# A first load cut into six transfers, a first head in six banks, and two convolution heads multiplied before the first turn

## The reference

```python
qkv = jnp.einsum('bsh,hf->bsf', x, w_qkv)            # 16 heads of 128 columns, q, k and v
scores = jnp.einsum('bhqd,bhkd->bhqk', q, k) / sqrt(128)
probs = softmax(scores)
values = jnp.einsum('bhqk,bhkd->bhkd', probs, v)     # column sums of probs times v
x = layernorm(x + einsum('bsf,fh->bsh', values, w_o))

kv = jnp.einsum('bhil,bhjl->bijhl', ctx, ctx)        # 16 heads of 8 channels
y = irfft(rfft(kv, 2L) * rfft(ssm_kernel, 2L))[..., :L] + kv * D
out = jnp.einsum('bijhl,bhil->bjhl', y, x)
x = layernorm(x + out)
```

## Time and profile before

| | us |
|---|---|
| median of 3 runs | 962.76 (962.2 to 966.51) |
| the profiled execution | 965.18 |
| its span | 963.4 |
| PE busy | 883.9 |
| DVE busy | 618.2 |

### The profile page before, as it was taken

The page is one execution under the profiler, slowest core; times in us unless marked ns, Lnnn a source line. Parts: engine busy times, 40 slices in busy tenths (PEclk is TensorE's granted clock), DMA queues, the critical chain, the costliest instruction groups (busy, mean ns, idle before and its releaser), DMA issues. The chain is left out here.

```text
span 963.4 us, 14009 instructions
## 1 busy us (share of the span) xinstructions
PE 883.9 (92%) x4408; PEld 633.9 (66%) x4408; DVE 618.2 (64%) x1169; ACT 395.9 (41%) x895; POOL 260.1 (27%) x246
## 2 busy tenths in 40 slices
PE   5999999999797799999999799999879889999995
PEld 4788888887444588888888575444454466555554
DVE  3666656666599654554554656888649988555554
ACT  1554565555411333233233322767630046555541
POOL 3122122120395022122212233111048641144200
PEclk9999999999698799999999989999979979999999
DMA  7011101101012111111112200000001013011001
GB/s 280 23 45 44 33 33 44 44 23 55 12 50 69 32 43 49 49 33 49 49 34 67 84 1 1 1 1 1 1 0 47 19 45 145 3 58 58 1 1 44
DMA packets 21752, 40.16 MB, mean 42 GB/s; under 512 B 2544, under 2 KB 13552, under 8 KB 20464
## 3 DMA queue, kind: packets, MB, share of 16 engines
q1 hardware_dynamic: 21712, 39.66, 12.8%
HBM read 38.60 MB, written 1.05 MB: 41 GB/s over the span
## 5 line engine op out<-in xcount | busy, mean ns | idle before, releaser
L1260 PE MATMUL bank<-xTh,ringh 128*128 128x512 f32 x432 | 176.7, 409 | 12.0 <-DVE xTl L873 11.2
L1261 PE MATMUL bank<-xTl,ringh 128*128 128x512 f32 x432 | 173.3, 401 | 0.0
L1262 PE MATMUL bank<-xTh,ringl 128*128 128x512 f32 x432 | 172.3, 399 | 0.0
L1260 PEld LDWEIGHTS bank<-xTh,ringh 128*128 128x128 f32 x432 | 83.1, 192 | 30.5 <-DVE xTl L873 11.2
L1262 PEld LDWEIGHTS bank<-xTh,ringl 128*128 128x128 f32 x432 | 82.4, 191 | 20.0
L1261 PEld LDWEIGHTS bank<-xTl,ringh 128*128 128x128 f32 x432 | 83.1, 192 | 15.3
L851 ACT ACTIVATE SF<-bank 128x512 f32<-128x512 f32 x108 | 64.5, 598 | 60.8 <-DVE HF L1237 30.7
L1237 DVE TENSOR_TENSOR HF<-bank,SF 128x512 f32<-128x512 f32 x96 | 63.5, 687 | 34.8 <-PE bank L1607 31.2
L1077 DVE TENSOR_TENSOR arena<-bank,arena 128x512 f32<-128x512 f32 x48 | 33.2, 691 | 73.0 <-PE bank L1262 73.0
L793 ACT ACTIVATE Eh<-arena 128x512 fp32r<-128x512 f32 x48 | 30.3, 632 | 115.4 <-DVE arena L1081 115.4
L1296 PE MATMUL bank<-outh,Eh 128*128 128x256 f32 x192 | 63.5, 331 | 1.4 <-DVE El L1085 1.4
(11 more groups left out here) (214 smaller groups left out, 2018.7 us busy)
## 6 DMA issues: line engine op xcount, KB each, us to landing
ring<-w_attn SPq DMA_DIRECT2D x16, 384.0 KB, 3.2
ring<-w_moe SPq DMA_DIRECT2D x24, 256.0 KB, 2.7
lowraw<-w_low SPq DMA_DIRECT2D x6, 1024.0 KB, 5.8
toep<-toep SPq DMA_DIRECT2D x32, 128.0 KB, 2.1
outring<-w_down SPq DMA_DIRECT2D x24, 128.0 KB, 2.0
outring<-wo_attn SPq DMA_DIRECT2D x16, 128.0 KB, 2.0
ring<-w_ffn SPq DMA_DIRECT2D x6, 256.0 KB, 5.0
wq<-w_attn SPq DMA_DIRECT2D x1, 1344.0 KB, 13.3
```

Source lines behind the costliest of these rows:

```text
L1260: pe.matmul(o, ringh[:, slot, wc], xTh[:, k, halves[j]], start=(k == 0), stop=False)
L1261: pe.matmul(o, ringh[:, slot, wc], xTl[:, k, halves[j]], start=False, stop=False)
L1262: ins = pe.matmul(o, ringl[:, slot, wc], xTh[:, k, halves[j]], start=False, stop=(k == DK - 1))
```

## The change

1. **Loads.** SP now issues the first half of the tokens of `xT`, then head 0's weights as q, k and v thirds with a semaphore each, then the second half of `xT`, then head 0's output weights. `consts` and the skip vector `dskip` move ahead of `xN`.
2. **Splits.** DVE casts and subtracts half by half and signals each of the two feature blocks (`x_high`, `x_low`). ACT casts head 0's weights in thirds, POOL subtracts them in thirds.
3. **First projections.** `project_first` does, for each of the six, the two high x high matmuls first, then the two with `ringl`, then the two with `xTl`, with waits of their own. The order is q, k, v of the first half, then of the second (`FIRST`), into six different banks (`FIRST_BANKS`).
4. **Convolution ahead.** PE does convolution head 0 in the last attention head, between `attn_out(14)` and `key_weights(15, 0)`, and head 1 after `attn_out(15)`, before the turn. POOL multiplies both heads' products as soon as the attention weights are split, into a part of `lowraw` (free until the second layer's feed-forward) instead of `kv`, and then adds the first four diagonals. From head 2 on POOL waits for `xt_act`, i.e. until the turn has ended.
5. **The room for it.** The turn writes banks 4 to 7. The first four `diag` are made by ACT before head 0 of the attention. In the last attention head ACT casts and DVE splits the output weights earlier.

```diff
-            sp.dma_start(xT[:], x_t.rearrange("(k p) t -> p k t", p=P)).then_inc(xt_in, 16)
+            def load_x(j):
+                half = slice(j * HALF, (j + 1) * HALF)
+                sp.dma_start(xT[:, :, half], x_t[:, half].rearrange("(k p) t -> p k t", p=P)).then_inc(xt_in[j], 16)
+            def load_first(part, signal):
+                cols = slice(part * D, (part + 1) * D)
+                sp.dma_start(ring[:, 0, cols], w_attn0[0, :, cols]).then_inc(signal, 16)
+            load_x(0)
+            load_first(0, first_in[0])
+            load_first(1, first_in[1])
+            load_first(2, ring_in[0])
+            load_x(1)
...
-            for h in range(2):
-                conv_fix(h, h)
             pool.wait_ge(ctx_in, 16)
-            pool.wait_ge(out0_banks, 4)
+            for h in range(2):
+                conv_products(0, h, h, cT, cT)
+            for h in range(2):
+                conv_fix(h, h)
             for h in range(CH):
-                conv_products(0, h, h % 2, cT, cT)
+                if h == 2:
+                    pool.wait_ge(xt_act, 4)
+                if h >= 2:
+                    conv_products(0, h, h % 2, cT, cT)
...
-            pe.wait_ge(x_split, 1)
-            for c in range(6):
-                project(0, 0, c)
+            def project_first(c):
+                part, j = c // 2, c % 2
+                o = bank[:, FIRST_BANKS[c], :]
+                pe.wait_ge(hi_first, part + 1)
+                for k in range(DK):
+                    pe.wait_ge(x_high, 2 * j + k + 1)
...
+            for c in FIRST:
+                project_first(c)
...
+                if isinstance(h, int) and h == NH - 1:
+                    pe.wait_ge(act_evac, 4 * NH)
+                    conv(0, 0, 0)
                 key_weights(h, 0)
...
             attn_out(NH - 1, 1)
-            def turn(layer_norm):
+            conv(0, 1, 1)
+            def turn(layer_norm, first_bank=0):
...
-                for h in range(4):
+                for h in range(2 - 2 * layer, 4):
                     conv(layer, h, h)
```

More of the change, by code:

```diff
@@ L723, in head @@
                 high_e(h, 1)
-                high_out(h, slot, out0_done, count(h - 1))
+                if not last:
+                    high_out(h, slot, out0_done, count(h - 1))
                 high_v(h, 0)
@@ L732, in _, with norm_and_turn @@
                 evac_q(0, 0, j)
-            for j in range(2):
                 evac_v(0, 0, j)
+            act.wait_ge(skip0_in, 16)
+            act.wait_ge(const_in, 16)
+            for h in range(4):
+                act.activation(diag[:, h, :], ident, ACT.Identity, scale=dskip[:, h:h + 1]).then_inc(diag_done, 1)
             two_at_a_time(act, NH, head)
-            def norm_and_turn(layer_norm, turn=True, high=False, lead=0):
+            def norm_and_turn(layer_norm, turn=True, high=False, lead=0, first_bank=0):
                 def deviations(j):
@@ L934, in head @@
                 low_e(h, 1)
-                low_out(h, slot)
+                if not last:
+                    low_out(h, slot)
                 scale_v(h, slot, 0)
@@ L1330, in head @@
                 ahead(5)
-            pe.wait_ge(x_split, 1)
-            for c in range(6):
-                project(0, 0, c)
+            def project_first(c):
+                part, j = c // 2, c % 2
+                o = bank[:, FIRST_BANKS[c], :]
+                pe.wait_ge(hi_first, part + 1)
+                for k in range(DK):
+                    pe.wait_ge(x_high, 2 * j + k + 1)
+                    wc = slice(part * D + k * P, part * D + (k + 1) * P)
+                    pe.matmul(o, ringh[:, 0, wc], xTh[:, k, halves[j]], start=(k == 0), stop=False)
+                if part < 2:
+                    pe.wait_ge(lo_first, part + 1)
+                else:
+                    pe.wait_ge(w_split, 1)
+                for k in range(DK):
+                    wc = slice(part * D + k * P, part * D + (k + 1) * P)
+                    pe.matmul(o, ringl[:, 0, wc], xTh[:, k, halves[j]], start=False, stop=False)
+                for k in range(DK):
+                    pe.wait_ge(x_low, 2 * j + k + 1)
+                    wc = slice(part * D + k * P, part * D + (k + 1) * P)
+                    ins = pe.matmul(o, ringh[:, 0, wc], xTl[:, k, halves[j]], start=False, stop=(k == DK - 1))
+                ins.then_inc(proj_done, 1)
+            for c in FIRST:
+                project_first(c)
             pe.wait_ge(ones_done, 1)
```

123 lines of the change are left out of this document (69 added, 54 removed).

## The result

The changed kernel takes 958.20 us (median of 10 runs, 952.77 to 960.63) against 962.77 (10 runs, 959.20 to 966.51) of the kernel before: 0.9946 of it, with 0.9924 to 0.9969 as 95% interval. A second comparison gave 957.79 against 962.33, 0.9939 (0.9918 to 0.9961). (The ratio and its interval are the record's, from all the runs of a comparison; the quotient of the two medians is 0.9953 both times.) So it is faster by about 5 us where 10.4 were forecast, and lies just above the range, which ended at 957.5. The profiled execution took 958.47, its span is 956.7.

A forecast was written before the change was run, and what follows sets the result against it. PE was taken to bound attention, with waits at the start and around the last head and turn. Terms -5.8 - 4.6 + 0.5 - 0.5 = -10.4 us took the profiled 965.18 to 954.8, median 952.4; range 948.0 to 957.5.

The forecast's parts named there:

- Head 2's split: Attention head 0: POOL's split of head 2's weights comes in head 0's time as before; no cost counted.
- POOL's products: Beside heads 14 and 15, 4 x 1.04 us: taken as 0, at most one product's 1.04 us.
- head 0 of the convolution before `key_weights`: Last attention head: three matmuls there put +0.5 us on the chain to the turn.
- The convolution: Behind the turn: 14 heads left for PE, first one cold, ending at 298.1; -4.6 us.
- Rival (c): Convolution: clock is up at head 2 and DVE bounds it, 39.5 us; total 950.2 us; chance 0.15.
- the cold case: Convolution starting at 1.2 GHz: 41.7 us from the turn's end to the last reduction instead of 46.35.
- The start: First projections: input and weights land in pieces, PE starts at 5.4 instead of 11.18; -5.8 us.
- The Trainium skill's figure for small transfers: Start: at 138 GB/s a third takes 0.95 us, PE starts at 6.0; the term would be -5.2.
- The turn: Norm before the turn: `ve` falls from 0.65 to 0.17, -0.5 us; convolution head 1 ahead of it counted 0.
- The forecast's own sign of error: Stages from the experts on: prediction is wrong if they change by over 2 us.
- rival (e): Later stages: further cold stretches of 2.7 us each, six make it slower, 968.6 us; chance 0.02.
- the forecast's step from profile to median (-2.4): Whole kernel: the profiled execution stood 2.4 above the median, so 954.8 became a median of 952.4 us.

The follow-up runs named there:

- Early_w2: The changed kernel with head 2's projection weights issued ahead of `xN`; 956.13 us, 0.9927 of the kernel before.
- split_late: The changed kernel with POOL's split of head 2's weights held until both `El` of head 0 are written; 956.63 us in 12 timed runs, 0.9929.
- quiet_short: The changed kernel with all transfers behind the second input half issued only once that half has landed; 958.2 us in a single run.
- quiet_long: The changed kernel with `xT` in two 4 KB-row transfers, head 0's weights in one, everything else issued after the second input piece landed; 956.5 us, single run.
- conv0_late: The changed kernel with convolution head 0 also behind `attn_out(15)`, with head 1; 955.17 us in one run.
- start_only: The changed kernel with only the new loads, six banks and casts in parts, products and convolutions put back as before; 958.24 us, 0.9965.

## Why the prediction missed

By its own terms, from the table of events (stage lengths, mean of before against mean of after):

| term | forecast | measured |
|---|---|---|
| start, to head 0's scores | -5.8 | -5.1 |
| head 0's chain ("Head 2's split comes in head 0's time as before") | 0 | +1.2 |
| from there to head 15's scores, with POOL's products | 0 | +0.3 |
| head 0 of the convolution before `key_weights` | +0.5 | +0.4 |
| `attn_out(15)` to the turn's end | -0.5 | -1.5 |
| convolution 0 | -4.6 | -2.3 |
| from there to the router | 0 | +0.3 |
| behind the router, to the ordinary run of before | 0 | +2.2 |
| sum | -10.4 | -4.5 |

**Head 2's split** is the step that failed in its reasoning. The forecast moved head 0 by 5.8 us and left POOL's split where it was, on the word "as before", though the earlier trace rows show the two side by side and the price of a hit. It did not ask what held the split either: PE's projections of head 0, which moved by 5.6 us, and close behind them a queued transfer, which came 1.4 us later. What had been a hit on the row maxima became one on the normalisation, on the chain to `key_weights`. The price the forecast named (1.04 at most) was for the new products. Early_w2, split_late and quiet_short each took the hit on head 0 away.

**The convolution** failed in its size. The mechanism is as told: 14 heads behind the turn, DVE nearly always busy, a cold start. But the 46.35 us on which the 4.6 rest were the longest of five executions: 44.98, 43.44, 44.90 and 43.43 followed. Before's second and fifth:

```profile
254.65:299.63 44.98, 43.01 (x96) 18.80 (x96) 39.68 (x64) 4.38 (x13) 38.07 (x46) 0.96 0.12 36
```

```profile
256.81:300.24 43.43, 41.47 (x96) 18.16 (x96) 39.66 (x64) 4.36 (x12) 38.09 (x46) 1.00 0.13 37
```

How much of the stage runs at 1.2 GHz decides. The parts of it at 0.50, in before's first and second execution and in the changed kernel:

```profile
256.34:262.00 5.66, 5.61 (x7) 2.51 (x8) 0.77 (x2) 1.16 (x5) 0.03 (x1) 0.50 0.00 0
```

```profile
254.65:257.00 2.35, 2.29 (x3) 1.17 (x4) 0.12 (x1) 1.16 (x5) 0.00 (x0) 0.50 0.00 0
```

```profile
251.94:259.00 7.06, 5.60 (x7) 2.52 (x8) 5.45 (x9) 1.95 (x6) 4.91 (x7) 0.50 0.00 1
```

Before had about 5.9, 3.2, 0, 3.0 and 0 us of it in its five executions, the changed kernel 7.0 and 6.5. At the full clock the stage takes 43.4 against 39.7 us, so the heads moved ahead save 3.8. With 6 to 7 us of it cold it takes 46.3 against 42.4 and 42.2, so they save 3.9 to 4.2, near the forecast's 4.6. Mean against mean only 2.3 are left, since the changed kernel meets more of the cold clock: the forecast took before's coldest execution for both sides. The clock falls at 248.7 and 246.8 in the changed kernel's two executions, and the turn's end now comes 3.2 and 3.8 us behind the fall, where in before it came 4.3 to 8.3 us behind. What sets the moment of the fall stays open. Rival (c)'s 39.5 us for a convolution at the full clock was right (39.66 and 39.68), but it came by itself in only three of the 12 profiles with heads ahead and no unused products (quiet_long, conv0_late, split_late). The forecast's 41.7 us for the cold case was 0.4 to 0.7 short: PE waits 1.46 for DVE before it can write the banks, where 1.06 were taken for POOL's product.

**The start** is 0.7 short, all in the landings: the first half at 5.38 instead of 4.6, and the first third of the weights, whose cast PE waits for last, at 5.7 instead of 4.9. The forecast gave pieces in flight side by side the rate of one large transfer. The Trainium skill's figure for small transfers (DMA: Bandwidth & Descriptors, Bandwidth) had led to PE at 6.0, and it came at 6.15. That is luck: this estimate had the first half at 4.6 and the third 0.95 us behind it, and measured are 5.38 and 0.3. The rest (casts, low parts without a stall, banks worth nothing) came as forecast. A projection was not 2.6 us long throughout, as reckoned there; all six took 10.34, so the low parts had less time than the forecast gave them and still came without a wait of note.

**The turn** gained 1 us more than forecast. From the start of `attn_out(15)` DVE reached its statistics after 3.67 us in before (242.43 to 246.10) and after 3.08 (239.23 to 242.31) in the changed kernel, whose products run at 2.4 GHz: -0.6, a thing the forecast had counted only for head 1. The rest fits POOL's products. The forecast looked at the one small operation that had been hit in its profile, `ve` at 0.65; `shift` beside it took 0.34, and before's fifth execution shows more:

```profile
246.77 2.03 POOL L520 TENSOR_TENSOR arena<-cT 128x512 f32<-128x512 f32 x2 [1.90 <-issue]
...
247.81 1.02 DVE L968 TENSOR_SCALAR ve<-mv 128x4 f32<-128x4 f32 x1
...
250.47 0.76 DVE L985 TENSOR_TENSOR shift<-nmean,rstd 128x4 f32<-128x4 f32 x1
```

Against 0.17 and 0.16 alone that is 0.85 + 0.60, where the first execution had 0.48 + 0.18; with no product near, all of it is gone. `attn_out(15)` ran at a granted clock of 1.00 in 11 of the 12 profiles with convolution head 0 ahead of `key_weights`, and at 0.50 to 0.68 in all seven without it (before, start_only, conv0_late). The exception is quiet_long with 0.65. So the filled wait goes with the full clock there, if not every time.

**The heads.** From the scores of head 1 to those of head 15 it takes 195.98 and 196.13 us against 195.62 to 195.64 in every execution of before and in start_only. All of it is in head 13, beside which the four products run (the forecast had them beside heads 14 and 15): from its scores to the next head's it takes 14.33 to 14.73 us in the 13 profiles with products ahead, and 13.97 to 13.99 in the six without. In the changed kernel:

```profile
204.25 4.47 POOL L541 TENSOR_TENSOR lowraw<-cT 128x512 f32<-128x512 f32 x4
...
207.99 1.29 DVE L931 TENSOR_TENSOR arena<-arena,rinv 128x512 f32<-128x512 f32 x1
```

It is the same second normalisation as in head 0, 1.29 us long instead of 0.69, at about a third of the 1.04 named as the most. In the table a shorter wait behind head 0's `key_weights`, which differs from execution to execution, takes 0.1 of it away.

**Behind the router.** The forecast's own sign of error, over 2 us in untouched stages, came only if the ordinary executions of before are taken (630.2 against 632.4). Then it is half of rival (e) without its size: not five or six cold stretches more, but one that is longer. Against the mean of the five executions, or against the first alone (632.1), the difference is 0.4 us or less. That the change causes it is not shown. Here the forecast's step from profile to median (-2.4) went wrong too: it took the surplus of one execution for a constant of both kernels, and in after the profiled one lies 0.3 above the median.

## What to carry to other kernels

When a stage moves forward, ask of each piece of work beside it what holds it, and what will hold it next (here a split that PE had released and that a queued load then held), and lay both timelines over each other: the hit wanders from a harmless instruction to one on the chain. Take the length of a stage that depends on the clock from several executions, or compare cold with cold; one profile gave this stage 3 us more than another. And after filling an idle stretch, look at the small gaps that are left beside it: with two unused products in each, the clock stayed up in the one profile taken, and the stage was 2.4 us shorter than in a cold execution of the kernel without them.

## What was not expected of the hardware

- Five executions of one stage with the same instructions (DVE busy 39.7 us in each) take 43.4 to 46.4 us; the stages behind the router 629.0 to 635.2, in steps near 629, 630.2, 632.4 and 635.
- From 3 to 5 us the DMA engines moved 281 to 318 GB/s with five pieces in rows of 1 and 2 KB, 302 and 334 with three pieces in rows of 3 and 4 KB, and 421 with `xT` in one transfer, though they are 0.90 to 1.12 busy in all of them.
- A DVE operation on 128 x 512 elements met by POOL's subtraction took 2.18 instead of 0.69 us and ended 0.54 after POOL's end at 25.15.
